# A two-layer attention kernel whose last item gets its own order on three engines

## The reference

```python
xn = layernorm(x, g_in)                        # 128 x 512
q = (xn @ Wq), 16 heads of 64; k, v = xn @ Wkv, one head for all 16
(k, v) = null key and null value in front      # 129 keys
sim = q @ k.T + bias, causal and key masks     # layer 1: q and k l2-normalised
attn = softmax(sim)
x = x + layernorm((attn @ v) @ Wo, g_out)
```

## Time and profile before

| | |
|---|---|
| Median of three runs | 1332.85 us (1330.36 to 1334.3) |
| The profiled execution | 1334.16 us, of which the span of its trace is 1332.4 us |
| TensorE busy | 1284.4 us (96% of the span) |
| VectorE, ScalarE, GpSimd busy | 1101.6, 861.7, 797.3 us |
| Granted TensorE clock, mean | 0.988 of full speed |
| Step 62, from its first scores matmul to that of step 63 (1284.22 to 1303.29 us) | 19.07 us, TensorE busy 19.07 us |
| Steps 63 and 64, to the end of the last matmul (1303.29 to 1327.12 us) | 23.83 us, TensorE busy 19.87 us |
| From there to the end of the span | 5.3 us |

### The profile page before, as it was taken

The page is one execution under the profiler, slowest core; times in us unless marked ns, Lnnn a source line. Parts: engine busy times, 40 slices in busy tenths (PEclk is TensorE's granted clock), DMA queues, the critical chain, the costliest instruction groups (busy, mean ns, idle before and its releaser), DMA issues.

```text
span 1332.4 us, 28554 instructions
## 1 busy us (share of the span) xinstructions
PE 1284.4 (96%) x8152; PEld 1183.8 (89%) x8152; DVE 1101.6 (83%) x2948; ACT 861.7 (65%) x3246; POOL 797.3 (60%) x1382
## 2 busy tenths in 40 slices
PE   3798999999999999999999999999999999999997
PEld 2587999999999999999999999999999999999995
DVE  5676877877777887887799999899899999999986
ACT  3565667666667777776666766666666666666663
POOL 6443444444445666554567776776766766776673
PEclk8898999999999999999999999999999999999999
DMA  9101411111123212213454101101111110110101
GB/s 286 35 19 50 78 44 47 36 35 47 47 96 111 86 59 96 102 58 112 110 129 174 49 24 47 47 31 39 47 36 34 47 45 26 47 47 24 47 33 40
DMA packets 52195, 85.67 MB, mean 64 GB/s; under 512 B 7888, under 2 KB 22256, under 8 KB 51616
## 3 DMA queue, kind: packets, MB, share of 16 engines
q1 hardware_dynamic: 47168, 75.81, 18.2%
q0 software_dynamic: 4128, 9.03, 2.3%
q10 hardware_dynamic: 832, 0.04, 0.0%
HBM read 57.07 MB, written 27.79 MB: 64 GB/s over the span
## 4 chain that ended last, share of the span: by engine, by line
PE 92%; DVE 3%; issue 2%; ACT 1%; SPq 1%; POOL 1%; DMA 0%; POOLq 0%; DVEq 0%; ACTq 0%
PE bank_q L1270 30%; PE bank_y L1406 26%; PE bank_s L1270 12%; PE bank_o L1270 10%; PE bank_p L1371 6%; PE bank_t L1344 4%; PE bank_t L1310 3%; ACT p_raw L799 1%; PE bank_t L1349 1%; DVE wq_raw L969 1%; PE bank_y L1270 0%; POOL bias L569 0%; SPq L367 0%; DMA bias<-in_fside_16xSxS 0%; DVE pt_l L1152 0%
## 5 line engine op out<-in xcount | busy, mean ns | idle before, releaser
L799 ACT ACTIVATE p_raw<-s_sb,neg_m 128x130 f32<-128x130 f32 (+1 forms) x1024 | 372.0, 366 | 134.7 <-DVE neg_m L1142 133.0
L641 POOL TENSOR_TENSOR p_sb<-p_raw,rden 128x256 f32<-128x256 f32 x256 | 157.6, 615 | 308.3 <-DVE rden L1148 308.3
L1270 PE MATMUL bank_q<-wq_h,xt_h 128*128 128x384 f32 x768 | 268.2, 349 | 4.4 <-DVE xt_l L1040 4.3
L1270 PE MATMUL bank_q<-wq_h,xt_l 128*128 128x384 f32 x768 | 260.0, 339 | 0.0
L1270 PE MATMUL bank_q<-wq_l,xt_h 128*128 128x384 f32 x768 | 259.8, 338 | 0.0
L631 POOL TENSOR_TENSOR bias_g<-bias,mask_row 128x260 f32<-128x260 f32 x256 | 178.5, 697 | 120.7 <-DVE s_sb L1135 119.2
L1406 PE MATMUL bank_y<-wo_h,ot_h 128*128 128x512 f32 x512 | 218.0, 426 | 0.3 <-DVE ot_l L1158 0.3
L1406 PE MATMUL bank_y<-wo_h,ot_l 128*128 128x512 f32 x512 | 201.8, 394 | 0.0
L1406 PE MATMUL bank_y<-wo_l,ot_h 128*128 128x512 f32 x512 | 201.5, 394 | 0.0
L799 ACT ACTIVATION_READ_ACCUMULATOR p_raw<-s_sb,neg_m 128x1 f32 x1024 | 192.5, 188 | 0.0
L1152 DVE TENSOR_TENSOR pt_l<-bank_p,pt_h 128x384 fp32r<-128x384 f32 x256 | 140.6, 549 | 37.4 <-ACT pt_h L806 37.4
(11 more groups left out here) (136 smaller groups left out, 3155.3 us busy)
## 6 DMA issues: line engine op xcount, KB each, us to landing
x_in<-in_x SPq DMA_DIRECT2D x32, 256.0 KB, 3.1
x_res<-in_x SPq DMA_DIRECT2D x32, 256.0 KB, 2.7
x_mid<-y_out SPq DMA_DIRECT2D x32, 256.0 KB, 2.1
x_in<-x_mid SPq DMA_DIRECT2D x32, 256.0 KB, 2.8
x_res<-x_mid SPq DMA_DIRECT2D x32, 256.0 KB, 2.7
out_x<-y_out SPq DMA_DIRECT2D x32, 256.0 KB, 2.1
wq_raw<-in_L_cond_Wq SPq DMA_DIRECT2D x4, 768.0 KB, 6.4
wq_store<-w_sb SPq DMA_DIRECT2D x6, 384.0 KB, 3.9
```

The costliest lines, as they stand in the source:

```text
L641: e.tensor_tensor(to[:, 0:2 * P].rearrange("p (e j) -> p e j", e=2), low_blocks(of)[:, :, 2:LOW], r[:, 0:2, :].broadcast_to([P, 2, P]), AL ...
L799: last = e.activation(p_raw[:, g % 2, lo:hi], s_sb[:, g % 2, lo:hi], ACT.Exp, bias=neg_m[:, h:h + 1], accum_out=esum[:, h:h + 1])
L1270: last = e.matmul(out, a, b, start=(k == 0), stop=(k == len(passes) - 1))
```

## The change

`stream` takes a further argument, `last_step`, and uses it in place of `step` for n of 63 and more. PE, DVE and ACT each get such a function; SP and POOL keep their `step`. Steps 0 to 62 are as before. The stages are the same ones and as many; only their order in steps 63 to 65 differs, and stages of items that don't exist there are left out of the lists.

```diff
--- before.py
+++ after.py
@@ -108,14 +108,14 @@
     return lambda d: ((n + d) // B, (n + d) % B) if 0 <= n + d < N else None
 
 
-def stream(e, step, between=None):
+def stream(e, step, between=None, last_step=None):
 
 
     def straight(first, last):
         for n in range(first, last):
             if between:
                 between(n)
-            step(item_of(n))
+            (last_step if last_step and n >= N - 1 else step)(item_of(n))
 
     straight(0, FIRST)
     for layer in range(LAYERS):
@@ -877,6 +877,23 @@
                     scale = g_in_sb[:, 1, c:c + 1] if kind == "q" else 1.0
                     e.activation(hi.bitcast(F32R), raw, ACT.Copy, scale=scale).then_inc(high_ready, 1)
 
+            def last_step(at):
+                def on(d, stage, *which):
+                    if at(d) is not None:
+                        stage(at(d), *which)
+
+                on(0, exps, 0)
+                on(0, exps, 1)
+                on(0, exps, 2)
+                on(0, split_pt, 0)
+                on(0, exps, 3)
+                on(-1, split_ot, 1)
+                on(0, split_v)
+                on(0, split_pt, 1)
+                on(0, split_pt, 2)
+                on(0, split_ot, 0)
+                on(0, split_pt, 3)
+
             first = (0, 0)
             project_weights(0, 0)
             split_xt(first)
@@ -889,7 +906,7 @@
             split_qt(first, 1)
             net_silu(GAIN1, EXP1)
             split_kt(first)
-            stream(e, step)
+            stream(e, step, last_step=last_step)
 
 
         @block.vector
@@ -1234,6 +1251,35 @@
                 if n == 3:
                     second_null()
 
+            def last_step(at):
+                def on(d, stage, *which):
+                    if at(d) is not None:
+                        stage(at(d), *which)
+
+                on(0, scores, 0)
+                on(0, maxima, 0)
+                on(0, scores, 1)
+                on(0, maxima, 1)
+                on(-2, y_center)
+                on(0, sums, 0)
+                on(0, scores, 2)
+                on(0, maxima, 2)
+                on(0, sums, 1)
+                on(0, scores, 3)
+                on(0, maxima, 3)
+                on(0, split_v)
+                on(0, split_pt, 0)
+                on(0, sums, 2)
+                on(-1, split_ot, 1)
+                on(-2, y_finish)
+                on(0, split_pt, 1)
+                on(0, sums, 3)
+                on(0, split_pt, 2)
+                on(0, split_ot, 0)
+                on(0, split_pt, 3)
+                on(-1, y_stats)
+                means_variances(at)
+
             first, second, third = (0, 0), (0, 1), (0, 2)
             x_stats(first)
             means_variances(item_of(-3))
@@ -1257,7 +1303,7 @@
             x_stats(third)
             means_variances(item_of(-1))
             net_silu(EXP1, PLUS1, REC1, [1, 2, 3])
-            stream(e, step, between)
+            stream(e, step, between, last_step)
 
 
         @block.tensor
@@ -1439,6 +1485,26 @@
                 on(0, transpose_p, 3)
                 on(0, net_second_transposes)
 
+            def last_step(at):
+                def on(d, stage, *which):
+                    if at(d) is not None:
+                        stage(at(d), *which)
+
+                on(0, scores, 0)
+                on(0, scores, 1)
+                on(-1, attend, 1)
+                on(0, scores, 2)
+                on(0, transpose_p, 0)
+                on(0, scores, 3)
+                on(-1, output, 0, 2)
+                on(0, transpose_p, 1)
+                on(-1, output, 2, 4)
+                on(0, transpose_p, 2)
+                on(-1, output, 4, 6)
+                on(0, attend, 0)
+                on(0, transpose_p, 3)
+                on(-1, output, 6, 8)
+
             first = (0, 0)
             transpose_x(first)
             for p in range(3):
```

## The result

Over seven runs each, the changed kernel takes 1337.51 us (1335.64 to 1340.73) and the kernel before 1333.0 us (1330.36 to 1335.66). The ratio is 1.0035, with a 95% interval of 1.0021 to 1.0050: slower by 4.7 us, with 2.8 and 6.7 us as the ends. The forecast was 1338.35 us, within 1334.6 to 1341.3.

What follows compares the result with a forecast made beforehand. TensorE was taken to bound the kernel, with 92% of the chain and about 3.9 us idle in the tail. At full clock +3.3 us, plus 2.2 for the low clock, gave +5.5: 1338.35 us, range 1334.6 to 1341.3.

Steps and rivals of the forecast that it cites:

- The front of step 63: Start of step 63: exps 2 about 0.9 us earlier, normalise 1 by 1.9 us; transpose_p 0 at 1309.12 instead of 1309.03.
- DVE stops at split_v: Step 63, DVE: stands still 2.9 us for ACT's split_v, with split_pt 0 and sums 2 queued behind.
- My +1.0 us for a kernel without this stall: Tail, if later stages could overtake the blocked split_v: about +1.0 us in sum.
- TensorE's wait: Step 63, ahead of transpose_p 1: TensorE waits from 1311.7 to 1315.9, 4.2 us, with outputs 2 to 8 queued behind.
- The late statistics: End of step 63: y_stats(62) and y_center come late, so the output of item 63 starts at 1324.6 instead of 1321.33.
- The sum at full clock: Whole tail with the granted clock staying up: +3.3 us, 0.25%, with bounds of +2.9 and +3.8.
- The clock: TensorE's granted clock falls in the 4.2 us wait or just behind it, likely low for 6.8 us: 2.2 us lost.
- The whole: Whole kernel: 3.3 + 2.2 = +5.5 us, median 1338.35 us, slower by 0.41%.
- The one of full clock: Rival for the tail: the wait is there, the clock stays up, +3.3 us, 1336.15 us; chance 0.26.
- The one of an earlier end: Rival for the tail: the earlier front brings the end sooner, time 1331.15 us; chance 0.04.
- The one of a low clock through the last output: Rival for the tail: clock falls and stays low 10 us, +7.9 us, 1340.75 us; chance 0.12.
- The moves costed at nothing: Last steps: y_finish(61), store of item 61 and load of x_res for item 62 come later; 5 us cover the load.

Runs made afterwards that it cites:

- e2: Changed kernel with DVE's split_v of the last step moved behind sums 3 instead of ahead of split_pt 0; ratio to before 1.0006, tail 25.13 us.
- e3: Changed kernel with ACT's order of the last steps as before, DVE and TensorE keeping the new one; ratio to before 1.0007, tail 24.38 us.
- e1: Changed kernel with 24 matmuls of unread result on TensorE ahead of transpose_p 1 of the last step; ratio to before 1.0019, tail 27.10 us.
- e7: Kernel with the study's own order of the last steps on ACT, TensorE and DVE; ratio to before 0.9974, tail 21.48 us.

## Why the prediction held, point by point

- **The front of step 63.** Right. exps 2 was put at 1309.2 and came at 1309.16 on the scale of before; transpose_p 0 at 1309.12, and came at 5.83 us into the tail, which is 1309.12.
- **DVE stops at split_v.** Right, and it is the step that carries the case: 2.9 us expected, 2.89 measured; its own split_v 0.75 us, the low end of what I allowed. e2 and e3, which take the stall away from either side, give 4.5 and 5.3 us back, 2.57 us of it by the clock (against e1, at full clock, it is 2.0 and 2.7 us). The Trainium skill, page TensorE: Matmul & The Clock Gate, section "Architectural detail: the array is 16× 32×32, not 1× 128×128", has these queues as strict first in, first out. The trace agrees: pt_h of group 0 waited 4.1 us behind a blocked stage that it had nothing to do with. My +1.0 us for a kernel without this stall compares with the +1.33 of e2, which is such a kernel.
- **TensorE's wait.** 4.2 us expected, 4.16 measured, and transpose_p 1 at 12.61 us into the tail, measured 12.63 (in one of three profiles 3.62 us and 13.50, after an earlier fall of the clock).
- **The late statistics.** Right: attend(63, 1) was put 19.5 us into the tail at full clock, and the filler kernel has 19.50; the wait for y_center was put at 0.6 us and is 0.41 to 0.43.
- **The sum at full clock.** +3.3 us expected, +3.30 in e1. Some of that is luck: the 0.2 us too many at y_center are made up by small amounts elsewhere.
- **The clock.** Right in kind: it fell in the wait, near 1315.0 on the scale of before. The term was too small in two of three profiles: 2.2 us reckoned, 2.57, 2.2 and 3.4 measured. The low stretch was 6.8 us as in the earlier trace rows; 5.1 to 5.9 us of it lay behind the wait, where my 2.2 us amount to 5.0. Of the 3.4 us, 0.9 came from a fall ahead of the long wait, which the prediction had no term for. The Trainium skill, on the same page, section "HAM oscillation — how this bites in real kernels" describes matmul bursts that run cold after each wait for data; the trace agrees here, with a granted clock of 0.50 behind the wait, and e1 shows that filling the wait prevents it.
- **The whole.** +5.5 us expected; the tails give +5.9, +5.5 and +6.7, the medians +4.5. The medians' interval reaches from 2.8 to 6.7 us and holds all three, but its middle is lower. Whether the kernel before pays for a low clock in some executions, which would explain it, is open.
- **The rivals.** The one of full clock is what e1 builds, and it was not the changed kernel. The one of an earlier end needed split_v off the path; e7 shows that such an order exists, but not this one. The one of a low clock through the last output did not occur; the profile with two falls comes nearest, at +6.7.
- **The moves costed at nothing.** On the scale of before, the loads of `x_res` for items 62 and 63 were issued 6.4 and 7.3 us later (1314.36 and 1326.06 us in the changed kernel's trace, 1311.15 and 1322.03 before), and no y_finish waited for one: the last one waited 0.16 us for POOL's inverse deviation, as it did before.

## What to carry to other kernels

An order written out by hand for several engines is one schedule. A stage that moves back on one engine (ACT's split_v behind exps 3) must not keep an early place on the engine that waits for it; write beside each stage when its input will be there, and look for the first one that is late. Work that is ready belongs ahead of work that must wait, above all on TensorE, where a wait costs its own length and can cost the low clock behind it as well. And for a change at one end of a kernel, measure from the trace the stretch that it touches: 5.9 us were plain there, while the whole time scatters by 5 us from run to run.

## What the runs showed of the hardware

The granted clock fell in TensorE's long wait in all three profiles of the changed kernel (4.16 us twice, 3.62 once). It also fell in or after single waits of 2.76, 2.40, 2.09 and 2.06 us, and once in a wait of 0.43 us behind one of 1.70. Of nine profiles with a wait of 2.06 to 2.09 us ahead of transpose_p 0, it fell there in two; in four with a wait of 2.0 us it stood. Low stretches lasted 3.4 us, or 6.8 us around the long wait. A wait of two microseconds is thus no safe length, and one and the same kernel gives different tails: 29.3 to 30.5 us in three profiles of the changed kernel, though 23.8 us each time in three of the kernel before. Matmuls whose result nobody reads, put in a wait, held the clock in both profiles (e1) and made the tail 2.6 us shorter, without a single useful operation starting earlier ahead of it.

The scatter of the whole kernel arises ahead of the store of item 3: over six profiles of the two kernels this store was issued between 160.66 and 165.41 us, while from there to step 63 all six needed 1137.5 to 1138.1 us.
